# A ring of six for gathered rows, and sixteen experts' second matrices kept on chip, in a chain of graph and expert layers

## The reference, cut to what matters

```
L0_ffn:  16 experts, 2 chosen:  y = relu(x @ w1[e] + b1[e]) @ w2[e] + b2[e]      (256 -> 512 -> 256)
L2_ffn:   8 experts, 1 chosen:  y = relu(x @ w1[e] + b1[e]) @ w2[e] + b2[e]      (256 -> 1024 -> 256)
L3_ffn:   6 experts, 2 chosen:  y = relu(relu(x @ w1[e] + b1[e]) @ w2[e] + b2[e]) @ w3[e] + b3[e]   (all 256)
x = x + sum over the chosen experts of weight * y
```

## Time and profile before

| | |
|---|---|
| runs | 6741.45, 6747.97, 6748.28 us; median 6747.97 us |
| the profiled execution's own time | 6698.96 us |
| its span in the trace | 6697.1 us |
| mean granted TensorE clock | 0.785 of full speed |
| busy: PE, PEld, DVE, ACT, POOL | 4506.5, 3138.6, 3363.6, 2539.8, 3081.5 us |
| moved by DMA | 727.93 MB, mean 109 GB/s |
| `block_experts`, first routed layer | about 1584 to 1971 us of the span |
| `block_experts`, second routed layer | about 5272 to 5525 us |
| `block_experts`, third routed layer | about 6390 to 6656 us |

### The profile page before, as it was taken

One profiled execution on the slowest core, in us unless ns is written; L12 is line 12 of the kernel. 1 busy time (PEld: TensorE's weight loads), 2 busy tenths in 40 slices (PEclk: granted clock), 3 DMA queues, 4 the chain that ended last, 5 costly groups with the idle time before them and its releaser, 6 DMA issues. The chain is left out here.

```text
span 6697.1 us, 62301 instructions
## 1 busy us (share of the span) xinstructions
PE 4506.5 (67%) x16614; PEld 3138.6 (47%) x16614; DVE 3363.6 (50%) x7195; ACT 2539.8 (38%) x5493; POOL 3081.5 (46%) x2991
## 2 busy tenths in 40 slices
PE   4799945556954777545556676996777592555665
PEld 2466634345743555212245343774555581333454
DVE  2344435554625666679744565225666315454522
ACT  2577723331212233355432443223333122666511
POOL 3276766652653666235500652004665124666244
PEclk7899966766986666679977788997777696677878
DMA  4433343334644555224330221004555353666245
GB/s 115 128 105 103 107 89 92 91 81 116 201 136 114 140 139 138 58 82 132 107 79 9 51 47 29 14 3 124 140 143 126 115 168 102 183 188 182 66 140 168
DMA packets 464743, 727.93 MB, mean 109 GB/s; under 512 B 173990, under 2 KB 334801, under 8 KB 453972
## 3 DMA queue, kind: packets, MB, share of 16 engines
q1 hardware_dynamic: 299372, 388.69, 20.0%
q0 software_dynamic: 161520, 330.66, 18.8%
q10 hardware_dynamic: 3530, 4.89, 0.2%
HBM read 592.07 MB, written 139.85 MB: 109 GB/s over the span
## 5 line engine op out<-in xcount | busy, mean ns | idle before, releaser
L593 PE MATMUL ps<-msg,same 128*125 128x256 f32 (+2 forms) x3328 | 1343.0, 548 | 883.9 <-issue 397.7
L593 PEld LDWEIGHTS ps<-msg,same 128*125 128x125 f32 x3328 | 773.1, 260 | 1297.8 <-issue 787.2
L569 POOL DMA_INDIRECT msg<-d_gat,src_i x832 | 794.1, 954 | 430.9 <-issue 197.0
L482 POOL DMA_INDIRECT rec<-rec,slot_i x391 | 415.8, 1063 | 299.5 <-PE ps_f L424 121.2
L569 POOL DMA_INDIRECT msg<-d_lin,src_i x416 | 394.2, 948 | 267.8 <-issue 101.9
L569 POOL DMA_INDIRECT msg<-rel_rows,src_rel x416 | 399.4, 960 | 213.5 <-issue 98.3
L645 ACT ACTIVATE same<-off 128x500 f32<-128x500 f32 x208 | 128.9, 620 | 865.8 <-PE ps L593 455.2
L424 PE MATMUL ps_f<-w,hs 128*128 128x256 f32 x1568 | 391.0, 406 | 27.1 <-DVE hs L462 26.3
L639 ACT ACTIVATE off<-ramp_r,minus_lo 128x125 f32<-128x125 f32 x1248 | 390.6, 384 | 10.9 <-PEq L58 10.9
L424 PEld LDWEIGHTS ps_f<-w,hs 128*128 128x128 f32 x1568 | 308.7, 202 | 145.8 <-DVE hs L462 74.9
L1566 ACT ACTIVATE hid<-ps_h,w 128x250 f32<-128x250 f32 x348 | 163.5, 470 | 531.8 <-PE ps_h L1525 508.6
(11 more groups left out here) (594 smaller groups left out, 9209.3 us busy)
## 6 DMA issues: line engine op xcount, KB each, us to landing
lo_rows<-lo_r SPq DMA_DIRECT2D x208, 256.0 KB
fil<-rec SPq DMA_DIRECT2D x104, 512.0 KB
rows<-bc_d SPq DMA_DIRECT2D x96, 447.0 KB
w<-in_L_ffn_packed SPq DMA_DIRECT2D x40, 1026.0 KB
w<-in_L_ffn_packed SPq DMA_DIRECT2D x16, 2052.0 KB
w<-in_L_ffn_packed SPq DMA_DIRECT2D x30, 770.0 KB
rel_rows<-row SPq DMA_DIRECT2D x25, 896.0 KB
lo_rows<-ffn_lo_r SPq DMA_DIRECT2D x32, 500.0 KB
```

Of the source, the lines that this page charges most:

```text
L482: nc.gpsimd.indirect_dma_start(k.rec, bass.IndirectOffsetOnAxis(slot_i[0:rows, c:c + 1], 0), rec[0:rows, g % R, j, :], None).then_inc(sent ...
L569: nc.gpsimd.indirect_dma_start(msg[:, g % R, j, :], None, table, bass.IndirectOffsetOnAxis(idx[:, n:n + 1], 0)).then_inc(msg_in[g % R], 16)
L593: nc.tensor.matmul(ps[:, j, 0:width], same[:, g % 2, j, :], msg[:, g % R, j, 0:width], start=True, stop=True).then_inc(mm, 1)
```

## The change

Three things change, all around `block_experts`.

1. The ring of gathered rows has six places instead of three, in all three routed layers: six gathers are issued ahead of the blocks, and then block `n`'s turn issues gather `n + 6`.
2. In the first routed layer alone (`sort` is set only there), the second matrices of all 16 experts are loaded once, 512 KB an expert and 8.4 MB in all, into a tile `second` that stays on chip through the layer. Eight of these loads are issued on SP's queue in `front` ahead of the stores of `tokens`, eight behind them. The packed load of a block then brings only the first matrix and the biases (`WIDE`), 514 KB in place of 1026 KB. `down(n)` on PE reads the block's expert number from `block_i` into a register, and its matmuls read `second` at an address made from that register. Before its first `down` PE waits once until all sixteen have landed.
3. The packed row is laid out anew (second matrix last), and one more stage encloses the stages of each routed layer, which adds an empty barrier at its end.

```diff
 def front(k, ..., also=(), kept=()):
                             sp.dma_start(to[lo:hi], of[lo:hi]).then_inc(moved, 16)
+                for to, of, landed in kept[0::2]:
+                    sp.dma_start(to, of).then_inc(landed, 16)
                 for g in range(GROUPS):
                     sp.wait_ge(rows_done, (g + 1) * STEP)
                     for lo, hi in SPLIT:
                         sp.dma_start(tokens_d[lo:hi, span(g), :], rows[lo:hi, span(g), :]).then_inc(moved, 16)
+                for to, of, landed in kept[1::2]:
+                    sp.dma_start(to, of).then_inc(landed, 16)
                 sp.wait_ge(moved, 32 * (GROUPS + len(also)))
...
 def block_experts(k, ..., to_i=None, second=None):
+    WIDE = x.at_w2 if second else x.width
+    LAST = x.width - x.at_w2
     R = 3
+    RR = 6
...
-        rows = s.sb("rows", [P, R, TB, D])
+        rows = s.sb("rows", [P, RR, TB, D])
-        w, b2 = s.sb("w", [128, R, x.width]), s.sb("b2", [P, R, D])
+        w, b2 = s.sb("w", [128, R, WIDE]), s.sb("b2", [P, R, D])
...
-                    sp.dma_start(w[:, b, :], x.packed[ds(e * 128, 128), :]).then_inc(w_in[b], 16)
+                    sp.dma_start(w[:, b, :], x.packed[ds(e * 128, 128), 0:WIDE]).then_inc(w_in[b], 16)
...
                 def down(n):
+                    if second:
+                        e = pe.value_load(block_i[0:1, n:n + 1], min_val=0, max_val=x.n - 1)
+                        weights = lambda c: second[0][:, ds(e * LAST + c * D, D)]
+                    else:
+                        weights = lambda c: w2(n, c)
...
-                            ins = nc.tensor.matmul(ps_o[:, t, 0:D], last[...], w2(n, c), start=c == 0, stop=c == count - 1)
+                            ins = nc.tensor.matmul(ps_o[:, t, 0:D], last[...], weights(c), start=c == 0, stop=c == count - 1)
...
                 up(0)
+                if second:
+                    pe.wait_ge(second[1], 16 * x.n)
...
                 def gather(n):
-                    if n >= R:
-                        pool.wait_ge(t_mm, n - R + 1)
+                    if n >= RR:
+                        pool.wait_ge(t_mm, n - RR + 1)
...
-                for n in range(R):
+                for n in range(RR):
                     gather(n)
...
-                    if n + R < blocks:
-                        gather(n + R)
+                    if n + RR < blocks:
+                        gather(n + RR)
...
-                front(k, rows, cols, ..., (oh, wt), router, also)
+        with stage(k) as s:
+            second, kept = None, []
+            if sort:
+                last = x.width - x.at_w2
+                second = (s.sb("second", [128, n_exp * last]), s.sem("second_in"))
+                for e in range(n_exp):
+                    kept.append((second[0][:, e * last:(e + 1) * last], x.packed[e * 128:(e + 1) * 128, x.at_w2:x.width], second[1]))
+                    front(k, rows, cols, ..., (oh, wt), router, also, kept)
```

More of the change, by code:

```diff
@@ L901, in _, with front @@
                 c.link(nc.vector.tensor_tensor(gate[:], oh1[:], oh2[:], ALU.add))
-def front(k, rows, cols, tokens_d, n_exp, w, bias, mode, choice, router=None, also=()):
+def front(k, rows, cols, tokens_d, n_exp, w, bias, mode, choice, router=None, also=(), kept=()):
     nc = k.nc
@@ L1439, in _, with block_experts @@
                         add(g - 2)
-def block_experts(k, table, token_i, result, block_i, x, blocks, sort=False, shift=None, to_i=None):
+def block_experts(k, table, token_i, result, block_i, x, blocks, sort=False, shift=None, to_i=None, second=None):
     nc = k.nc
@@ L1482, in block_experts @@
         ps_t, ps_h, ps_o = s.ps("ps_t", [128, 2, 512]), s.ps("ps_h", [128, 4, 512]), s.ps("ps_o", [P, 2, 512])
-        w_in, rows_in = ([s.sem(f"{n}{j}") for j in range(R)] for n in ("w_in", "rows_in"))
+        w_in, rows_in = [s.sem(f"w_in{j}") for j in range(R)], [s.sem(f"rows_in{j}") for j in range(RR)]
         stored = [s.sem(f"stored{b}") for b in range(2)]
@@ L1510, in turn @@
                         for half in range(2):
-                            ins = nc.tensor.transpose(ps_t[:, n % 2, half * BR + t * P:half * BR + (t + 1) * P], rows[:, n % R, t, half * 128:(half + 1) * 128], k.ident[0:P, 0:P])
+                            ins = nc.tensor.transpose(ps_t[:, n % 2, half * BR + t * P:half * BR + (t + 1) * P], rows[:, n % RR, t, half * 128:(half + 1) * 128], k.ident[0:P, 0:P])
                     ins.then_inc(t_mm, 1)
@@ L1543, in down @@
                         for c in range(count):
-                            ins = nc.tensor.matmul(ps_o[:, t, 0:D], last[:, n % 2, c, t * P:(t + 1) * P], w2(n, c), start=c == 0, stop=c == count - 1)
+                            ins = nc.tensor.matmul(ps_o[:, t, 0:D], last[:, n % 2, c, t * P:(t + 1) * P], weights(c), start=c == 0, stop=c == count - 1)
                         ins.then_inc(o_mm, 1)
@@ L1677, in __init__ @@
         self.at_wm = 2 * f
[L1678 to L1679 removed]
+        self.at_b1 = self.at_wm + (2 * D if wm else 0)
         self.at_bm = self.at_b1 + f // 128
[L1681 removed]
+        self.at_w2 = self.at_bm + (2 if wm else 0)
+        self.width = self.at_w2 + (2 if wm else f // 128) * D
 class Experts:
@@ L3122, in routed @@
             tensor("token_i", [P, 2 * blocks + 2], I32) as token_i, tensor("to_i", [P, 2 * blocks], I32) as to_i, tensor("block_i", [1, blocks], I32) as block_i:
[L3123 to L3127, removed]
+        with stage(k) as s:
[5 more added lines that the diff above has]
+                    kept.append((second[0][:, e * last:(e + 1) * last], x.packed[e * 128:(e + 1) * 128, x.at_w2:x.width], second[1]))
+            with tensor("oh", [P, chosen, NT, n_exp]) as oh:
+                with nc.sbuf_tensor(f"cols_{x.f}_{n_exp}", [128, 2, N], F32) as cols:
+                    front(k, rows, cols, k.tokens.rearrange("(t p) f -> p t f", p=P), n_exp, gate_w, gate_b, mode, (oh, wt), router, also, kept)
+                route(k, (oh, wt), slot_i, block_i, token_i, to_i, n_exp, chosen, blocks, capacity)
+            block_experts(k, k.tokens, token_i, answered, block_i, x, blocks, sort, norm and norm[1], to_i if chosen == 2 else None, second)
         if chosen == 2:
```

11 lines of the change are left out of this document (5 added, 6 removed).

## The result

| | before | after |
|---|---|---|
| median of 4 runs each | 6748.12 us (6741.45 to 6750.31) | 6638.63 us (6633.74 to 6650.63) |
| ratio, 95% interval | | 0.9842 [0.9825, 0.9859] |
| profiled execution, span | 6698.96, 6697.1 | 6650.63, 6648.9 |
| first routed layer, block stage | 392.4 | 342.7 |
| second routed layer, block stage | 259.4 | 261.5 |

Forecast was 6640. Stages are counted from barrier to barrier, by the events of L58 on SP; the three new barriers (48 such events in place of 45) are in the stages' times.

A forecast was written before the change was run, and what follows sets the result against it. It took PE to bound the second routed layer, waits for loads and rows plus POOL's tail the first, a chain of waits the third. Terms -50 - 60 + 2 = -108 us from median 6747.97 gave 6640, range 6612 to 6682.

The forecast's parts named there:

- Third routed layer, -60: Third block stage: six places end 52.7 us of row waits, POOL then paces at 6.2 us a block; gain 60 us.
- First routed layer, -50: First block stage: row waits go, load stalls and slow matmuls cost 8 us for 40.8, POOL ends it; gain 50 us.
- Half the packed load: First block stage: a block's load shrinks from 8.15 to 5 us and is hidden, leaving one 5 us stall at block 3.
- Register read, 2 us: PE, first routed layer: about 0.8 us of sequencer per block, 40 times, mostly covered by queued matmuls; cost 2 us, bounds 0 and 32.
- Loads into `second`, 0: Front stage, first routed layer: 8.4 MB at 136 GB/s, eight issues fitting ahead of the stores of `tokens`; cost 0.
- Barriers and the second layer: Three more barriers cost 1 us, small things 1; second routed layer 0 as PE is full, start moving by 1 either way.
- Carrying the profiled difference over to the median: Whole kernel: the -108 us, worked out against the profiled 6698.96 us, was applied to the median 6747.97 us, giving 6640.
- Rival 1: Third routed layer turns to its loads at a 201 GB/s ceiling: gain 41 instead of 60, 6659 us; chance 0.13.
- Rival 2: First routed layer: the register read shows in every block, 11 to 32 us in all, 6670 us; chance 0.11.
- Rival 3: First routed layer: the last bias's load lands no earlier, so its waits stay; gain 15 to 20, 6672 us; chance 0.10.
- Rival 4: First routed layer: gaps at the register read hold TensorE's clock low, up to 291 us more, 6931 us; chance 0.04.
- Rival 5: Whole change: no effect, both layers' row waits returning at full length as waits of another kind; chance 0.02.

The follow-up runs named there:

- first set: First of three sets of follow-up runs, beside the kernel before on the same chip: before again 6169.05 us, changed kernel again 6072.64 us, ratio 0.9838.
- loads_ring4: Changed kernel with four places instead of three for packed weights and last biases in the third routed layer: 6069.31 us, 0.9827 of the kernel before.
- keys128: Changed kernel with only the first routed layer's keys load on 128 partitions instead of 125, biases still on 125: 6581.35 us, 0.9831 of the kernel before.
- ring4: Changed kernel with four places for gathered rows in place of six: 6603.72 us, 0.9866 of the kernel before.
- second_only: Changed kernel with the second matrices kept on chip but the ring of gathered rows at three as before: 6145.66 us, 0.9959 of the kernel before.

## Why the prediction was right, point by point

- *Third routed layer, -60.* Right; -57.1 with the extra barrier, -63.7 in the first set. POOL's pace was 6.21 us a block for 6.2 taken, and the last six blocks and stores took 6603.83 - 6570.14 = 33.7 us for 36 less the lead. `loads_ring4` shows that POOL sets the floor (6.12). That 6.21 came out so near is in part luck: it holds some 2 us of POOL's gaps, while PE waited for loads, which this term had at nothing.
- *First routed layer, -50.* Right; -49.7. Block 0's answers came 29.5 us behind the barrier (31.4 before, 3 less expected), the 31 blocks took 234.7 us for 233.4, the tail 73.1 for 75. The parts inside the term were less clean: the stall at block 3 was 7.74 us, not 5, since I had scaled it with the bytes, while `keys128` makes it vanish with more bytes; the slow `up` behind it cost 1.4 for 2, and the other load waits were 0 for 1. The errors nearly cancel, which is luck. I also took the waits for rows as a matter of asking early enough; `ring4` and the traces of before show that the late ones stand behind `order_d`.
- *Half the packed load.* `second_only` gives it 20.8 us, and with it alone the load waits inside the first layer are down to the one at block 3 (5.8 us). What I had not said is that the ring alone would bring more of them (31.4 us for 24.0).
- *Register read, 2 us.* Right that it is covered: 0 at one and at four reads. A read's row in after:

```profile
L1548 PEldq TENSOR_LOAD <-block_i x40: 296/310/492, 1629.1 to 1916.8; - x40
```

  Where the sequencer had just been held by a wait for rows, the read does show: `second_only` has 3.7 us of such idle time at `down` in all, up to 1.24 at once. With four places it is 0.5 us in all and with six none, so the deeper ring also keeps the read free.
- *Loads into `second`, 0.* The size was right, the working wrong. The eight issues did not fit ahead of the first store: they took 12.46 us, more than half of it in one of them, and the stores came 8.8 us later. I also had VectorE busy until about 1560 before, where the stage ended at 1547.8. It cost nothing, since VectorE ends the stage after, at 1571.15, behind the last of SP's issues at 1565.72: 5.4 us to spare, and the stage took 44.2 us in both traces. The traffic was 132 GB/s for 136 forecast, and `down` of block 0 didn't wait.
- *Barriers and the second layer.* 1.3 us for three barriers against 1; the second layer +2.1 with its barrier, +3.1 in the first set, outside the 1 allowed. Of the 3.1 the barrier is 0.3, and the wait for the first rows 1.3 (27.5 us for 26.2; 27.2 with the ring alone, 26.3 with three places); the rest stays open.
- *Carrying the profiled difference over to the median.* It held (-108 forecast, -109.5 measured). The 49 us by which before's profiled execution lay under its runs were a matter of that execution, and had I compared the two profiled spans alone I'd have read a gain of 48.
- *Rival 1* (loads): its ceiling of 201 GB/s didn't hold, 210 were moved here and 231 in the first set. Its waits did appear, 13.5 us, which was my sign of being wrong. They cost part of the stage, 2 to 9 us by the traces side by side (`loads_ring4`), and not the 19 that the rival had. *Rival 2*: excluded, since four reads a block show nothing. *Rival 3*: out in the first layer, where the bias ended no wait but the one at block 3, and that one went with the keys' load alone; the bias on 125 partitions does cost some 4 us in the second layer (261.3 to 256.9), where the rival didn't look. *Rival 4*: not at one read. *Rival 5*: excluded.
- *The range.* Its ends aren't what the terms named for them give: the lower one, with all 40.8 us gone and the third layer at 6.13 us with the lead in full, is 6640 - 8 - 5 = 6627 and not 6612; the upper one is 6672 (rival 3) or 6676 (rival 2 with a third of 1), not 6682. The measured 6639 lies inside either way.

## What to carry to other kernels

When two waits alternate on one engine, removing one alone brings part of the other out: price each part alone and both together. Where an engine's operation count times its pitch gives the stage's end, the order of the operations changes almost nothing; move them out of the full stretch or drop them. A wait that a trace shows on a load may be slack: one more buffer tells, by whether the time or only the releaser's name changes. Read it against several traces of the same code, since one stage can scatter from trace to trace by more (207.0 to 214.7 us here) than the buffer is worth.

## What the runs showed of the hardware

- *A broadcast onto 125 partitions held up another load; onto 128 it didn't.* With the keys' load on 128 partitions the stall at block 3 (7.1 to 8.1 us in six traces) went, at 2.4% more bytes, and the stage lost 7.9 us, with the bias's load changed too 10.6. With the bias on 128 partitions PE waited 21.2 and 21.3 us for the second layer's first rows in two traces, against 25.7 to 27.5 in the twelve others. By the rule of the Trainium skill, "DMA: Bandwidth & Descriptors", section "Why a DMA increments its semaphore by 16 and not by 1", an outer size of 125 goes on 5 engines and one of 128 on 16; the runs agree, but show only the effect and not the engines.
- *The same program took 6168 and 6175 us in two sets and 6691 to 6748 in the others.* Nearly all of it lies in stages that gather or scatter rows of edges (577.5 for 626.8 us in the one that makes the records, 548.4 for 626.4 in the next), and POOL's gathers there take as long themselves (954 and 952 ns each for `msg<-d_gat`). The row of the page for the matmuls of the edge sums, before, after, and before in the first set:

```profile
L593 PE MATMUL ps<-msg,same 128*125 128x256 f32 (+2 forms) x3328 | 1343.0, 548 | 883.9 <-issue 397.7
```

```profile
L593 PE MATMUL ps<-msg,same 128*125 128x256 f32 (+2 forms) x3328 | 1343.2, 549 | 916.8 <-issue 343.7
```

```profile
L593 PE MATMUL ps<-msg,same 128*125 128x256 f32 (+2 forms) x3328 | 1291.2, 542 | 598.7 <-DMA msg<-rel_rows,src_rel 223.1
```

  The idle time ahead of them differs by 285 us. What is slower wasn't found. The gain of the change was the same share in both: 0.9842 and 0.9838.
- *After a gap of about 5 us in every block the matmuls behind it ran at 0.57 to 0.65 of their pace* (3.62 us against 6.32 and 5.61), and the gap recurs every 15 us. The granted clock was 0.50 in the first 3 us behind such a gap. With the gaps gone it stood at 1.00.
